# Router logits and ranks issued one level later in a delta-rule recurrence, and a broadcast made by transposes

## The chip, the cores and the metric

The kernel runs on one NeuronCore of a Trainium2 chip. The metric is the device time of one execution in microseconds: the median of 3 runs. The span of a profile is the time from its first to its last instruction. TensorE is called PE here, VectorE DVE, ScalarE ACT, GpSimd POOL and SyncE SP, as in the profile.

## The reference, cut to what matters

x is 4096 tokens of 256 channels, fp32. Four blocks follow one another, each added to x: a delta-rule attention, a mixture of 8 experts with the best 2 of them per token, an RWKV time mix with a channel mix, and a ternary feed-forward net. The change touches the first block and the router of the second:

```
# block 1, per token t (heads fast and slow; the decay per step is a scalar)
pred = (q @ fH + q @ sH) / 2 ; u_neu = sigmoid(sum((v - pred)**2)) > 0.7
fH   = a*fH + (1-a)*(k v^T - k (k @ fH)) ; sH likewise, gated by importance
ns   = ns + u_neu*(nu - ns)*0.1                    # the neuron state
o    = p0*(q @ fH) + p1*(q @ sH) + p2*ns ; x += rmsnorm(o) @ Wo.T
# block 2, the router
logits = layernorm(x) @ w_router ; weights = two largest of softmax(logits)
x += sum over the two chosen experts of weight * mlp_expert(layernorm(x))
```

To send rows to experts the kernel needs, for each token, its logits, its two experts, and its rank among the tokens that chose the same expert (the row it gets in that expert's list).

## The kernel before, in words

**Tiling.** Tokens are cut into 32 chunks of 128 and 8 blocks of 512 (4 chunks). The recurrence is solved chunk by chunk in closed form: within a chunk the inverse of a triangular matrix is applied by 7 levels of repeated squaring. A turn handles two chunks, j = 0 and 1, interleaved; there are 16 turns, u = 0 to 15, from about 100 to 505 us of the span. All code is written out; each engine runs its own list in order, and semaphores alone tie the lists.

**A level on PE** (`level`) is, for j = 0 and then j = 1: four squarings (L1150, L1151), and two multiplications of the matrix into X (L1158, the "X multiplication"). ACT copies the squares out of PSUM (L889), DVE adds the product to X (`apply`, L533). Level 0 of a turn waits, ahead of its first X multiplication, until DVE has done all applies of the turn before:

```
                    elif not first:
                        pe.wait_ge(ap_rdy, t * (2 * LEVELS))
```

**Between the levels** PE does what belongs to the last turn (`y_transposes` L1166, `y_state` L1176, `predict` L1182 to L1186) and to the next (`transposes` L1128, `grams` L1134), and, by a table of stages in `turn`, the work on the block of 512 tokens behind the recurrence. `at(u, parity, lag, stage)` runs a stage in turns of one parity for block (u - lag)/2. In an odd turn: `gate_columns` (L1195) at level 0, `neuron_back` (L1202) and `z1_columns` (L1254) at levels 4 and 5, `logits` (L1212) behind level 6. In an even turn: `o_columns` (L1221) at level 0, `output` (L1230) at level 2, `ranks` (L1240 to L1243) behind level 6. So logits stand at the seam from an odd to an even turn, ranks at the seam from an even to an odd one.

**What they wait for.** `logits` of block b needs both halves of the transposed rows, the second of which ACT copies (`columns`, L943) late in the turn, behind the squares of DVE's new outputs (L911); it also waits until DVE has read bank 5. `ranks` needs DVE to have added the output of the next block (`residual`, L613), which frees bank 7, late in the even turn.

**DVE and ACT.** DVE, in an even turn: apply 0, `fold_words` (L570), `take_logits` (L640), `choose(b, 0)`, apply 1, and so on. In an odd turn: apply 0, `fold_words`, `gates` (L663 to L666), `take_ranks` (L671), `variances` (L625, L627), apply 1. ACT, in an odd turn: squares of level 0, `yt` (L896), `norm_root` (L930, which waits for `variances`), and only then the squares of level 1. At the end of an even turn DVE does `masks` (L520, L523), `residual` (L613), apply 6, `fold_words`, `neuron_gates` (L574, L575) and `stats` (L620); at the end of an odd turn `masks`, `outputs` (L595), apply 6, `fold_words`, `mean_squares` (L601, L602). The multiplications L1134 of `grams` release these masks.

**Behind the turns** stand, in order and on one chain, the last blocks' stages, until POOL has scattered the rows of block 7 (L307) and the experts begin.

Of the kernel before, what the change touches and what calls it, by code (L numbers as in the profile page):

```python
# [16 lines left out]
S, D, DS, HID, NE = 4096, 256, 64, 1024, 8  # L17
CH = 128
# [55 lines left out]
def build(nc, A):  # L74
# [5 lines left out]
    with ctx:  # L80
# [10 lines left out]
        def bank(name):  # L91
            return ctx.enter_context(nc.psum_tensor(name, [128, 512], fp32))
# [14 lines left out]
        def sb(name, shape, dt=fp32, to=None):  # L107
            return (to or ctx).enter_context(nc.sbuf_tensor(name, shape, dt))
# [10 lines left out]
        small = sb("small", [128, 16, NC])  # L119
# [81 lines left out]
        B = [bank(f"bank{i}") for i in range(8)]  # L201
# [80 lines left out]
        NG_, VE, NM, M1, M2, UB, RKU = IMP, RK, RQ, P0, P1, RSTD, RST1  # L282
# [8 lines left out]
        def bank_of(b, item):  # L291

            return (bank_behind if b == LAST else bank_in_turns)[item]


        def block_of(u, parity, lag):

            b = (u - lag) // 2
            return b if u % 2 == parity and u >= lag and b < NB else None
# [754 lines left out]
        def _(pe):  # L1054
            T = nc.tensor
            I_ = ident[:, :]
            pe.wait_ge(mk_rdy, 2)
            for m in range(2):
# [3 lines left out]
                last = T.matmul(B[6][:, 2 + m:3 + m], one_m[0:1, :], pw_s[0:1, m, 128:129], start=True, stop=True)  # L1062
# [11 lines left out]
            def neuron_out(b):  # L1074
                pe.wait_ge(ld_v, 16)
                pe.wait_ge(hd_rdy, b + 1)
                if b >= 1:
                    pe.wait_ge(nu_out, b)
                T.matmul(B[7][0:DS, :], nm2T[:, :], hT[:, :], start=True, stop=True).then_inc(nu_ps, 1)
# [58 lines left out]
            def level(t, p, n, first):  # L1138
                for j in range(2):
                    if n == 0:  # L1140
                        pe.wait_ge(l_rdy, t * 2 + (j + 1))
                        pe.wait_ge(x_rdy, t * 2 + (j + 1))
                    else:
                        pe.wait_ge(sq_cp, t * (2 * LEVELS - 2) + (2 * (n - 1) + j + 1))
                    Ln = L[:, p, j, n % 2, :, :]
                    if n < LEVELS - 1:
                        for m in range(2):
                            a, b_ = Ln[:, 2 * m, :], Ln[:, 2 * m + 1, :]
                            if n < LEVELS - 2:
                                T.matmul(B[j][:, 256 * m:256 * m + 128], b_, a, start=True, stop=True)  # L1150
                            last = T.matmul(B[j][:, 256 * m + 128:256 * m + 256], a, b_, start=True, stop=True)  # L1151
                        last.then_inc(sq_ps, 1)
                    if n > 0:
                        pe.wait_ge(ap_rdy, t * (2 * LEVELS) + (2 * (n - 1) + j + 1))
                    elif not first:
                        pe.wait_ge(ap_rdy, t * (2 * LEVELS))
                    for m in range(2):
                        last = T.matmul(B[2 + j][:, 0:256].rearrange("p (a m d) -> p a m d", a=2, m=2)[:, :, m, :],  # L1158
                                        Ln[:, 2 * m + 1, :], X[:, p, j, :, m, :], start=True, stop=True)
                    last.then_inc(ap_ps, 1)  # L1160

            def y_transposes(t, p):
                pe.wait_ge(ap_rdy, (t + 1) * (2 * LEVELS))
                pe.wait_ge(pp_rdy, t * 2 + 1)
                for j in range(2):
                    last = T.transpose(B[6][:, j * 128:(j + 1) * 128], X[:, p, j, 1, :, :].rearrange("p m d -> p (m d)"), I_)  # L1166
                last.then_inc(yt_ps, 1)
# [3 lines left out]
            def y_state(t, j):  # L1171
                c = t * 2 + j
                pe.wait_ge(yt_rdy, t + 1)
                pe.wait_ge(f_rdy, c + 1)
                pe.wait_ge(pp_rdy, c + 1)
                T.matmul(B[6][:, 256:384], YT[:, j, :], both, start=True, stop=True).then_inc(w_ps, 1)  # L1176

            def predict(t, p, j):
                c = t * 2 + j
                pe.wait_ge(lq_rdy, c + 1)  # L1180
                pe.wait_ge(w_rdy, c + 1)
                T.matmul(B[6][:, 0:128], KQT[:, p, j, 3, :], both, start=True, stop=False)  # L1182
                w = Wb[:, j, :]
                for m in range(2):
                    T.matmul(B[6][:, m * DS:(m + 1) * DS], QM[:, p, j, m, :], w[:, half[m]], start=False, stop=m == 1)
                T.matmul(B[6][:, 384:512], KR[:, p, j, :, :].rearrange("p m d -> p (m d)"), w,  # L1186
                         start=True, stop=True).then_inc(pp_ps, 1)

            def gate_columns(b):
                pe.wait_ge(ng_rdy, b + 1)  # L1190
                if 1 <= b < LAST:
                    pe.wait_ge(x1_rdy, 2 * b - 1)
                for j in range(CPB):
                    c = b * CPB + j
                    last = T.matmul(B[bank_of(b, "gate")][0:DS, j * CH:(j + 1) * CH], small[:, NG_, c:c + 1].broadcast_to([128, DS]), I_,  # L1195
                                    start=True, stop=True)
                last.then_inc(gc_ps, 1)

            def neuron_back(b):
# [6 lines left out]
            def logits(b):  # L1206
                pe.wait_ge(z1T_rdy, 2 * b + 2)
                if b + 1 < LAST:
                    pe.wait_ge(o_rdy, b + 2)
                for j in range(CPB):  # L1210
                    for k in range(KT):
                        last = T.matmul(B[bank_of(b, "logits")][:, j * NE:(j + 1) * NE], zT[:, 0, k, j * CH:(j + 1) * CH], wroT[:, k, :],  # L1212
                                        start=(k == 0), stop=(k == KT - 1))
                last.then_inc(lg_ps, 1)

            def o_columns(b):
                pe.wait_ge(o_rdy, b + 1)
                if 1 <= b < LAST:
                    pe.wait_ge(z1T_rdy, 2 * b)
                for j in range(0, CPB, 2):  # L1220
                    last = T.transpose(B[bank_of(b, "o")][:, j * DS:j * DS + 128], ot[:, j:j + 2, :].rearrange("p c d -> p (c d)"), I_)  # L1221
                last.then_inc(ot_ps, 1)
# [34 lines left out]
            def at(u, parity, lag, stage, *args):  # L1257
                b = block_of(u, parity, lag)
                if b is not None:
                    stage(b, *args)  # L1260

            def turn(u):

                t, p, deltas, head, tail = u, u % 2, u < TURNS, u + 1 < TURNS, 1 <= u <= TURNS
                for n in range(LEVELS):
                    if deltas:
                        level(t, p, n, not tail)
                    if tail:
                        if n == 0:
                            y_transposes(t - 1, 1 - p)  # L1270
                        elif n == 1:
                            y_state(t - 1, 0)
                        elif n == 2:
                            predict(t - 1, 1 - p, 0)
                        elif n == 3:
                            y_state(t - 1, 1)
                        elif n == 4:
                            predict(t - 1, 1 - p, 1)
                    if head:
                        if n in (0, 4):  # L1280
                            transposes(t + 1, 1 - p, n // 4)
                        if n in (2, 5):
                            grams(t + 1, 1 - p, n // 3)
                    if u == 0 and n == 1:
                        neuron_out(LAST)
                        project(NB, 0)
                    if n == 0:
                        at(u, 0, 4, o_columns)
                        at(u, 1, 3, gate_columns)
                    elif n == 2:  # L1290
                        at(u, 0, 4, output)
                    elif n == 4:
                        at(u, 1, 3, neuron_back)
                        at(u, 1, 5, z1_columns, 0)
                    elif n == 5:
                        at(u, 1, 5, z1_columns, 1)
                    elif n == 6:
                        at(u, 1, 5, logits)
                        at(u, 0, 6, ranks)

            z_transposes(0)
            for i in range(NB):
# [20 lines left out]
                turn(u)  # L1323
            t, b5, b6, b7 = TURNS - 1, LAST - 2, LAST - 1, LAST
            y_transposes(t, t % 2)
            o_columns(b6)
            y_state(t, 0)
            predict(t, t % 2, 0)
# [1501 lines left out]
```

## Time and profile before

| | |
|---|---|
| median of 3 runs | 2169.77 us (2169.62 to 2170.21) |
| profiled execution | 2177.72 us, span 2175.9 us |
| PE busy over the span | 90% |
| DVE, ACT, POOL busy | 62%, 45%, 11% |
| mean granted clock of PE | 0.949 |
| the 16 turns | about 100 to 505 us of the span |
| from the turns to the first expert matmul | 505 to 581 us |

The profile is of one execution. Starts and durations of single instructions can be read from its trace; ends of PE instructions are modelled and overlap the next start, so PE's pace is better read from start to start. "Idle before" is the time in which the engine stood still ahead of an instruction, with what released it. The granted clock is 1.00 at 2.4 GHz and 0.50 at 1.2 GHz.

### The profile page before, as it was taken

The page shows a single profiled execution, that of the slowest core. Times are in us where ns is not written, and L with a number is a line of the kernel's source. Part 1 is how long each engine was busy: PE and PEld are TensorE (multiplying, and loading weights), DVE is VectorE, ACT ScalarE, POOL GpSimd, SP SyncE. Part 2 cuts the span into 40 slices and gives each one's busy share as a digit, 9 for nine tenths or more (in the row PEclk, how much of TensorE's full clock was granted, in tenths as well). Part 3 has the DMA queues.
Part 4 walks back from the last instruction along what each step waited for, and adds up shares of the span by engine and source line. Part 5 has one row for each costly group of instructions (what it writes and reads, how often), then busy time and mean ns, then how long its engine had stood idle before and what let it go on. Part 6 is the DMA issues. An engine that isn't in the chain of part 4 may idle for free. (4 is left out here: it accounts for less than half of the span.)

```text
span 2175.9 us, 32550 instructions
## 1 busy us (share of the span) xinstructions
PE 1965.3 (90%) x11554; PEld 1682.8 (77%) x11554; DVE 1354.6 (62%) x2760; ACT 975.4 (45%) x1777; POOL 247.8 (11%) x229
## 2 busy tenths in 40 slices
PE   7999999997399999996776749998999999999999
PEld 5799999996399999996544437776888888888887
DVE  7566677776466666665799877886345345344442
ACT  4655555553234444342788656662232233223221
POOL 0010012222333223232000000000000000000000
PEclk9999999996699999998888869999999999999999
DMA  3299311112444433223232331414000000000000
GB/s 102 85 357 408 113 48 57 57 58 98 154 88 101 87 78 79 49 42 70 69 88 60 94 98 58 174 68 155 1 20 1 19 19 0 20 19 0 20 10 11
DMA packets 86100, 170.36 MB, mean 78 GB/s; under 512 B 7216, under 2 KB 49840, under 8 KB 85808
## 3 DMA queue, kind: packets, MB, share of 16 engines
q1 hardware_dynamic: 65920, 132.47, 17.5%
q0 software_dynamic: 18176, 33.70, 7.7%
q10 hardware_dynamic: 1888, 2.67, 0.4%
q8 instruction: 69, 1.13, 0.2%
q14 instruction: 47, 0.39, 0.1%
HBM read 91.61 MB, written 88.74 MB: 83 GB/s over the span
## 5 line engine op out<-in xcount | busy, mean ns | idle before, releaser
L2642 ACT ACTIVATE x_tok<-bank,scl 128x512 f32<-128x512 f32 x128 | 88.3, 690 | 360.2 <-PE bank L2693 359.4
L2692 PE MATMUL bank<-hAh,ffn_h 128*128 128x512 f32 x512 | 202.7, 396 | 0.7 <-DVE x_tok L2570 0.7
L2692 PE MATMUL bank<-hBh,ffn_h 128*128 128x512 f32 x512 | 201.7, 394 | 0.0
L2693 PE MATMUL bank<-hAl,ffn_h 128*128 128x512 f32 x512 | 199.4, 389 | 0.0
L2693 PE MATMUL bank<-hBl,ffn_h 128*128 128x512 f32 x512 | 199.3, 389 | 0.0
L1475 POOL DMA_INDIRECT tokens_behind_spare_rows<-yg,row_of_token x72 | 133.1, 1848 | 318.5 <-DVE row_of_token L1635 298.3
L889 ACT ACTIVATE L<-bank 128x512 f32<-128x512 f32 x160 | 94.5, 595 | 139.4 <-PE bank L1151 129.6
L533 DVE TENSOR_TENSOR st<-st,bank 128x256 f32<-128x256 f32 x224 | 90.6, 419 | 99.7 <-PE bank L1158 87.6
L1151 PE MATMUL bank<-L 128*128 128x128 f32 x768 | 146.9, 281 | 0.0
L1158 PE MATMUL bank<-st,L 128*128 128x128 f32 x896 | 139.3, 282 | 4.7 <-DVE st L533 4.7
L1572 ACT ACTIVATE h<-bank,b1s 128x256 f32<-128x256 f32 x280 | 125.5, 471 | 36.3 <-PE bank L1403 29.3
L2551 DVE CAST hBh<-x_tok 128x1024 fp32r<-128x1024 f32 x48 | 33.3, 694 | 157.6 <-ACT x_tok L2642 157.0
L1150 PE MATMUL bank<-L 128*128 128x128 f32 x640 | 130.5, 286 | 0.0
L2551 DVE CAST hAh<-x_tok 128x1024 fp32r<-128x1024 f32 x48 | 33.3, 693 | 148.7 <-ACT x_tok L2642 148.2
L1158 PEld LDWEIGHTS bank<-st,L 128*128 128x128 f32 x896 | 120.4, 197 | 6.5 <-DVE st L533 5.2
L1151 PEld LDWEIGHTS bank<-L 128*128 128x128 f32 x768 | 117.3, 197 | 0.1
L1558 ACT ACTIVATE yg<-yt,own_gates 128x256 f32<-128x256 f32 x70 | 31.7, 501 | 183.6 <-DVE yt L1630 176.9
L2692 PEld LDWEIGHTS bank<-hAh,ffn_h 128*128 128x128 f32 x512 | 96.1, 188 | 22.8 <-ACTq L2645 1.4
L2693 PEld LDWEIGHTS bank<-hAl,ffn_h 128*128 128x128 f32 x512 | 96.1, 188 | 21.8 <-issue 1.9
L2692 PEld LDWEIGHTS bank<-hBh,ffn_h 128*128 128x128 f32 x512 | 96.1, 188 | 21.3 <-ACTq L2645 1.4
L2693 PEld LDWEIGHTS bank<-hBl,ffn_h 128*128 128x128 f32 x512 | 96.1, 188 | 21.3 <-issue 1.4
L2692 PE MATMUL bank<-fTh,ffn_w 128*128 128x512 f32 x256 | 100.7, 393 | 6.9 <-ACTq L2615 6.9
(434 smaller groups left out, 5494.7 us busy)
## 6 DMA issues: line engine op xcount, KB each, us to landing
z_by_expert<-zero SPq DMA_DIRECT2D x64, 520.0 KB, 15.8
ckb<-in_ffn_dram POOLq DMA_DIRECT2D x32, 352.0 KB, 3.4
xg<-z_by_expert SPq DMA_DIRECT2D x36, 260.0 KB, 3.1
x_tok<-in_w_dram SPq DMA_DIRECT2D x8, 1024.0 KB
ffn_h<-ffn_copy SPq DMA_DIRECT2D x2, 4096.0 KB, 14.9
x_tok<-after_time_mix SPq DMA_DIRECT2D x15, 512.0 KB, 6.0
st<-in_w_dram SPq DMA_DIRECT2D x6, 1024.0 KB, 6.4
x_tok<-x_T SPq DMA_DIRECT2D x9, 512.0 KB, 4.2
```

What stands on the lines that cost most here:

```text
L533: V.tensor_tensor(x_, x_, B[2 + j][:, 0:256], ALU.subtract if n == 0 else ALU.add).then_inc(ap_rdy, 1)
L889: A_.activation(L[:, p, j, (n + 1) % 2, :, :], src, ACT.Copy).then_inc(sq_cp, 1)
L1150: T.matmul(B[j][:, 256 * m:256 * m + 128], b_, a, start=True, stop=True)
L1151: last = T.matmul(B[j][:, 256 * m + 128:256 * m + 256], a, b_, start=True, stop=True)
L1158: last = T.matmul(B[2 + j][:, 0:256].rearrange("p (a m d) -> p a m d", a=2, m=2)[:, :, m, :], Ln[:, 2 * m + 1, :], X[:, p, j, :, m, :], st ...
L1475: pool.indirect_dma_start(x2_d, bass.IndirectOffsetOnAxis(to_row[:, j:j + 1].bitcast(u32), 0), yg[:, j, :], None, compute_op=ALU.add).then ...
L1558: nc.scalar.activation(yg[:, j, :], yt[:, j, :], ACT.Copy, scale=own_g[:, 0, 0, j:j + 1]).then_inc(y_rdy, 1)
L1572: nc.scalar.activation(h32[:, m, :], B[m % 4][:, 0:TT], ACT.Gelu_apprx_tanh, bias=b1s[:, e * KH + m:e * KH + m + 1]).then_inc(h_act, 1)
L2551: go(V.tensor_copy(dst[0][:, m:m + 2, :], src))
L2642: A_.activation(gq[:, m % 4, :], B[2 + m % 4][:, :], ACT.Gelu, scale=scl[:, off[nm] + m:off[nm] + m + 1]).then_inc(g_act, 1)
L2692: T.matmul(out, w, x[0], start=first, stop=False)
L2693: return T.matmul(out, w, x[1], start=False, stop=last)
```

## The change

`gate_columns` made each of its four 64 x 128 products by a matmul of a broadcast column with the identity; it now makes a 128 x 128 transpose of the column broadcast to 128. ACT still reads the first 64 rows. `logits` moves from behind level 6 of the odd turn to behind level 0 of the next even turn, and `ranks` from behind level 6 of the even turn to behind level 0 of the next odd turn; `logits` of block 5, whose new place would be turn 16, is issued behind the turns. Nothing moves on the other engines.

```
             def gate_columns(b):
...
                     c = b * CPB + j
-                    last = T.matmul(B[bank_of(b, "gate")][0:DS, j * CH:(j + 1) * CH], small[:, NG_, c:c + 1].broadcast_to([128, DS]), I_,
-                                    start=True, stop=True)
+                    last = T.transpose(B[bank_of(b, "gate")][:, j * CH:(j + 1) * CH], small[:, NG_, c:c + 1].broadcast_to([128, 128]), I_)
...
                     if n == 0:
+                        at(u, 0, 6, logits)
+                        at(u, 1, 7, ranks)
                         at(u, 0, 4, o_columns)
                         at(u, 1, 3, gate_columns)
...
-                    elif n == 6:
-                        at(u, 1, 5, logits)
-                        at(u, 0, 6, ranks)
...
             y_transposes(t, t % 2)
+            logits(b5)
             o_columns(b6)
             y_state(t, 0)
```

PE at the seam from an odd to an even turn (turn 5 to turn 6): two pieces of the difference, the end of the odd turn and the place behind level 0 of the even one. The lines of functions further down are numbered one less in the changed kernel, so L1212 is L1211 there.

```order
 L1134 MATMUL bank<-st 128x128 x3
-L1254 MATMUL bank<-ident,Z 128x128 x4
+L1253 MATMUL bank<-ident,Z 128x128 x4
 L1158 MATMUL bank<-st,L 128x2x64 x4
-L1212 MATMUL bank<-small_weights,zT 128x8 x8
 L1150 MATMUL bank<-L 128x128
 L1151 MATMUL bank<-L 128x128
```

```order
 L1166 MATMUL bank<-ident,st 128x128 x2
 L1128 MATMUL bank<-ident,st 128x128 x3
-L1221 MATMUL bank<-ident,big 128x128 x2
+L1211 MATMUL bank<-small_weights,zT 128x8 x8
+L1220 MATMUL bank<-ident,big 128x128 x2
 L1150 MATMUL bank<-L 128x128
```

The last X multiplications of a turn are now followed at once by the squares of the next. The eight logits matmuls stand behind the transposes for the next turn.

PE in the first odd turn that has ranks (turn 7), behind its level 0:

```order
 L1166 MATMUL bank<-ident,st 128x128 x2
 L1128 MATMUL bank<-ident,st 128x128 x3
-L1195 MATMUL bank<-ident,small 64x128 x4
+L1239 MATMUL bank<-mask,tri 128x32
+L1240 MATMUL bank<-seen,one_m 128x32
+L1242 MATMUL bank<-mask,one_m 128x24
+L1242 MATMUL bank<-mask,one_m 128x16
+L1242 MATMUL bank<-mask,one_m 128x8
+L1195 MATMUL bank<-ident,small 128x128 x4
 L1150 MATMUL bank<-L 128x128
```

The five rank matmuls come ahead of the four transposes that replace the four gate matmuls.

PE behind the last turn:

```order
 L1166 MATMUL bank<-ident,st 128x128 x2
-L1221 MATMUL bank<-ident,big 128x128 x2
+L1211 MATMUL bank<-small_weights,zT 128x8 x8
+L1220 MATMUL bank<-ident,big 128x128 x2
 L1176 MATMUL bank<-state,YT 128x128
```

Block 5's logits now stand between the last transposes of Y and the state product that the last two chunks wait for.

## Rows read from the trace of the kernel before

**Rows 1.** Waits of PE, 100 to 505 us: line, releaser, us, times, longest.
```profile
PE bank L1212 <- ACT zT L943: 7.0, 5, 1.4
PE bank L1240 <- DVE x_tok L613: 4.8, 5, 1.0
```

**Rows 2.** Timeline, PE, seam of turns 13 and 14: start, us, line, count.
```profile
446.55 0.93 PE L1134 MATMUL bank<-st 64*128 64x128 f32 x6
...
450.36 1.95 PE L1212 MATMUL bank<-small_weights,zT 128*128 128x8 f32 x16 [1.40 <-ACT zT L943]
452.16 0.47 PE L1150 MATMUL bank<-L 128*128 128x128 f32 x2
...
453.14 0.61 PE L1158 MATMUL bank<-st,L 128*128 128x128 f32 x4
```

**Rows 3.** Timeline, PE, two earlier seams without logits or ranks.
```profile
180.36 0.93 PE L1134 MATMUL bank<-st 64*128 64x128 f32 x6
...
183.89 0.71 PE L1158 MATMUL bank<-st,L 128*128 128x128 f32 x4 [0.62 <-DVE st L533]
...
203.73 0.93 PE L1134 MATMUL bank<-st 64*128 64x128 f32 x6
...
207.29 0.71 PE L1158 MATMUL bank<-st,L 128*128 128x128 f32 x4 [0.64 <-DVE st L533]
```

**Rows 4.** Timeline, PE, first seam with ranks, and two later starts of ranks.
```profile
256.74 0.93 PE L1134 MATMUL bank<-st 64*128 64x128 f32 x6
...
259.73 0.38 PE L1240 MATMUL bank<-mask,tri 128*128 128x32 f32 x2 [0.97 <-DVE x_tok L613]
...
261.81 0.61 PE L1158 MATMUL bank<-st,L 128*128 128x128 f32 x4
...
312.51 0.38 PE L1240 MATMUL bank<-mask,tri 128*128 128x32 f32 x2 [0.97 <-DVE x_tok L613]
...
366.98 0.38 PE L1240 MATMUL bank<-mask,tri 128*128 128x32 f32 x2 [0.97 <-DVE x_tok L613]
```

**Rows 5.** Windows: stretch; length, busy PE, PEld, DVE, ACT, POOL; clock, DMA, GB/s.
```profile
423.40:426.70 3.30, 3.30 (x18) 3.30 (x17) 1.72 (x5) 0.89 (x2) 2.39 (x4) 0.50 0.57 184
```

**Rows 6.** Timelines of PE, DVE and ACT, end of turn 12, start of 13.
```profile
418.43 0.93 PE L1134 MATMUL bank<-st 64*128 64x128 f32 x6
...
421.19 0.74 DVE L533 TENSOR_TENSOR st<-st,bank 128x256 f32<-128x256 f32 x2
...
424.76 0.42 DVE L533 TENSOR_TENSOR st<-st,bank 128x256 f32<-128x256 f32 x1
427.12 0.42 DVE L533 TENSOR_TENSOR st<-st,bank 128x256 f32<-128x256 f32 x1 [1.94 <-issue]
...
430.77 0.21 ACT L930 ACTIVATE small<-small 128x4 f32<-128x4 f32 x1 [1.75 <-DVE small L627]
...
431.58 0.42 PE L1150 MATMUL bank<-L 128*128 128x128 f32 x2
```

**Rows 7.** Timeline, PE, turn 13: the gate's matmuls and four transposes.
```profile
427.56 1.09 PE L1195 MATMUL bank<-ident,small 128*64 128x128 f32 x8
...
444.17 0.66 PE L1254 MATMUL bank<-ident,Z 128*128 128x128 f32 x4
```

**Rows 8.** Timeline, DVE, turn 14: the logits taken, and apply 1.
```profile
456.26 0.18 DVE L640 COPY LG<-bank 128x32 f32<-128x32 f32 x1
...
458.82 0.75 DVE L533 TENSOR_TENSOR st<-st,bank 128x256 f32<-128x256 f32 x2
```

**Rows 9.** Timelines of PE and DVE behind the turns.
```profile
505.65 0.69 PE L1166 MATMUL bank<-ident,st 128*128 128x128 f32 x2 [0.73 <-issue]
...
507.20 0.79 PE L1176 MATMUL bank<-state,YT 128*128 128x128 f32 x2 [0.43 <-ACT YT L896]
...
520.27 0.68 DVE L580 SCALAR_TENSOR_TENSOR big<-bank,NU 64x512 f32<-64x512 f32 x1 [0.16 <-ACT big L907]
...
533.30 3.58 PE L1212 MATMUL bank<-small_weights,zT 128*128 128x8 f32 x16 [0.69 <-ACT zT L943]
```

More of the change, by code:

```diff
@@ L1194, in gate_columns @@
                     c = b * CPB + j
-                    last = T.matmul(B[bank_of(b, "gate")][0:DS, j * CH:(j + 1) * CH], small[:, NG_, c:c + 1].broadcast_to([128, DS]), I_,
-                                    start=True, stop=True)
+                    last = T.transpose(B[bank_of(b, "gate")][:, j * CH:(j + 1) * CH], small[:, NG_, c:c + 1].broadcast_to([128, 128]), I_)
                 last.then_inc(gc_ps, 1)
@@ L1287, in turn @@
                     if n == 0:
+                        at(u, 0, 6, logits)
+                        at(u, 1, 7, ranks)
                         at(u, 0, 4, o_columns)
@@ L1296, in turn @@
                         at(u, 1, 5, z1_columns, 1)
-                    elif n == 6:
-                        at(u, 1, 5, logits)
-                        at(u, 0, 6, ranks)
             z_transposes(0)
@@ L1325, in _ @@
             y_transposes(t, t % 2)
+            logits(b5)
             o_columns(b6)
```

## Prediction, on record before the changed kernel was run

> **What bounds the kernel now.** I read the busy table of the page first: PE leads with 90% of the span. Then the windows over the sixteen turns, then PE's waits there, then timelines around each wait. In the turns PE stands still at few places: 7.0 us ahead of five of the logits groups, for ACT's copy of the transposed rows, and 4.8 us ahead of five groups of ranks, for DVE's residual [rows 1]. Between these, PE is issued without a break, so PE is the bound there and time saved on it is time saved, as long as DVE and ACT follow.
>
> The reader should see a second cost behind the waits. The granted clock of PE falls to 0.50 (1.2 GHz) for 3.4 us and comes back. The windows show five such falls between 230 and 500 us; [rows 5] is one, all 18 PE records of it stretched. One comes 3 us after the first logits wait, the other four about 2 us after the waits of the second to fifth ranks. What one costs is read from the pace: from the first ranks to the second 52.78 us pass without a fall between them, from the second to the third 54.47 us with one [rows 4]; the difference is 1.7 us. I use 1.65, since the other pairs lie at 54.44.
>
> I measure from S, the start of a turn's last Gram group (L1134), because DVE's work at the seam starts from it.
>
> **Seam from odd to even turn (logits), five times.** Before: S is 446.55, the logits start at 450.36 after 1.40 idle and hold PE until 452.16, which is 1.80; the first X multiplication of the next turn starts at 453.14, or S + 6.59 [rows 2]. After: the logits are gone from here, and that multiplication waits for DVE's apply 6. Two earlier seams show this without logits or ranks: S + 3.53 behind `outputs`, with 0.62 idle, and S + 3.56 behind `residual`, with 0.64 idle [rows 3]. So the wait does not vanish; it shrinks and moves into level 0. The logits cost their 1.80 later all the same. Gain: 6.59 - 1.80 - 3.53 = 1.26 each, 5 x 1.26 = 6.3 us. Their data is then long there, as ACT's copy lies ahead of its next squares.
>
> **Seam from even to odd turn (ranks), five times.** Before: from S = 256.74 to the X multiplication at 261.81 is 5.07 [rows 4]. The ranks in it are 10 passes of PE, 1.1 us at the logits' pace (1.80 for 16). After: S + 3.56. Gain at the seam: 5.07 - 1.1 - 3.56 = 0.4. The wait for DVE hardly shrinks, since the same DVE work that delayed the ranks now delays the X multiplication.
>
> **Gate broadcast.** Eight passes last 1.09 us, four transposes in the same stretch 0.66 [rows 7]: a matmul of fp32 is issued as two passes, a transpose as one. With the tail of the last pass, which is paid in either case, taken off, the eight hold PE for about 1.0 and the four for 0.5, so 0.5 is saved per block. In turns 3 and 5, which have no ranks, that is all PE time: 1.0 us. In turn 7 it adds to the 0.4: 0.9 us.
>
> In turns 9 to 15 something else ends last. ACT's copy of the squares of level 1 stands behind L930, which waits for DVE's variances, and those stand behind apply 0, the fold, the gates and the ranks taken. From DVE's second apply of level 0 (427.12) to PE's level 2 (431.58) are 4.46 us, with ACT's L930 at 430.77 in between [rows 6]. After the change DVE sets the pace to there: apply 6 at S + 2.76 (421.19 - 418.43), the first apply of level 0 3.57 later (424.76), the second 0.35 behind it, and then 4.46: S + 11.1. Before it was 431.58 - 418.43 = 13.15 [rows 6], of which 1.65 is the fall of the clock. So 2.0 us are gained where no fall remains, and only 0.35 of these belong to the moved ranks and the gate; DVE takes the rest. Four such turns, the last with a shorter stretch before (12.9): 7.8 us. With turn 7: 8.7 us.
>
> **The clock.** Those 7.8 us contain four falls; the fifth, in turn 6, is 1.65 more. That they go is my choice, and the largest one. What the trace shows is that falls followed long gaps: 1.40 idle, or 0.97 idle with the short rank passes directly behind it, and that the two seams of [rows 3], 0.62 and 0.64 idle, were followed by none. After the change the gaps are 0.4 to 0.9, and full squares and X multiplications (1.8 us) stand between the gap and the short passes.
>
> The Trainium skill speaks against this. "TensorE: Matmul & The Clock Gate", Part 4, says that work in transpose mode does not count as PE being busy for the clock. By that rule the change puts transposes (Y, next turn, gate) right beside the logits and the ranks and makes two stretches per pair of turns that look idle. The z1 transposes of [rows 7] already stand a few us ahead of the logits gap and no fall followed in four of five cases, so the trace leans against it without settling it; what it would do is the last rival below.
>
> **DVE's new wait for the logits.** `take_logits` finds them ready today; afterwards it waits until PE is through level 0, five transposes and the logits, and `choose`, apply 1 and the rest of the turn queue behind it. From the copy to apply 1 are 2.56 us [rows 8], to the end of its first half 3.0. PE needs that half at the X multiplication of level 2: 1.80 of logits, 0.2, a level of 2.7, 0.2 and 0.9 of squares, 5.8 us after the logits begin. DVE gets there 1.95 (duration of the logits in [rows 2]) + 0.1 + 3.0 = 5.05 after. So 0.7 us of cover is left, and I book nothing. `take_ranks` comes behind gates that are later than the ranks: nothing.
>
> **Behind the turns.** Block 5's logits used to run while PE waited for apply 6. Now they lie between Y's transposes (505.65) and the state product (507.20) [rows 9]. At the low clock, which [rows 9] show for the same 16 passes, they take 3.58; less the wait for YT that they cover, 0.43 and part of the 0.6 before it, I take 2.9 us, all on the chain to the experts. Bounds: at full clock 1.8 less 1.1 = 0.7; at the low clock with nothing covered, and a later return of the full clock, 4. The eighth gate is shortened from two passes to one too, but DVE waited only 0.16 for it (L580) [rows 9]: -0.2.
>
> **Sum.** -6.3 - 1.65 - 8.7 - 1.0 + 2.9 - 0.2 = -15.0 us. The profiled execution goes from 2177.7 to 2162.7. It is 7.9 above the median of the runs, which I take as the same for both: 2169.8 - 15.0 = 2154.8, said as 2155. All phases behind are shifted, not changed. About 0.2%, 4.3 us, is what a measurement here can tell from no change.
>
> **Rivals.**
> - *The falls of the clock stay*, one per pair of turns, since gaps remain at every seam. For it: 0.97 idle was enough before, and the even-to-odd gap stays near 0.9. Against: the gap and the short passes are parted. The seams give 6.3 + 5 x 0.4, the gates 1.5 at most where DVE does not hide them, the tail -2.7: 2169.8 - 7 = 2163.
> - *DVE becomes the bound of the even turns.* The 0.7 of cover at `take_logits` is used up where POOL's scatters stretch DVE's small operations, and each of five turns loses about 1 us: 2155 + 5 = 2160.
> - *Slower: two falls per pair.* If stretches with transposes and short passes let the clock fall, both seams of all five pairs have them (the skill's rule as a mechanism of this kernel). Ten falls of 1.65 instead of none: 2154.8 + 16.5 = 2171.3. The point from which it decides is nine falls (15.0 / 1.65). For it: at the odd-to-even seam transposes, logits and o_columns make 2.6 us in a row. Against: 3.2 us of idle and logits in a row caused one fall in five before.
> - *The change does not do what it says*: logits or ranks could be held by another semaphore at the new place. Those they wait for (ACT's copy, DVE's residual and outputs) are all set in the turn before, so I give it no weight of its own.
>
> **Numbers.** Forecast 0.60; falls stay 0.18; DVE-bound even turns 0.12; ten falls 0.05; the rest (a few falls, or other losses behind the turns) 0.05. The forecast's own range is 2151 to 2159, from the bounds of the tail and one fall more. The range for 8 in 10 is 2150 to 2164, which takes in both milder rivals. Faster by over 0.2% is below 2165.4: the first three cases nearly whole, 0.88; within 0.2%: 0.09, most of it the ten falls; slower by more: 0.03.
>
> **What would show it.** In the profile after: no idle ahead of the logits and ranks; 0.4 to 0.9 idle ahead of the first X multiplication of turns 6 to 15, released by DVE L533; the X multiplication at S + 3.5; level 2 of odd turns at S + 11.1; ranks 51.1 us apart; granted clock 1.00 from 130 to 500 us; the gate with 4 records in place of 8; behind the turns the state product 2.9 us later against the turn's end. A clock of 0.50 anywhere in turns 6 to 15, or a PE wait at level 2 of even turns, would make the forecast wrong.

## The result and the profile after

The changed kernel takes 2149.1 us (median of 4 runs, 2148.87 to 2150.3); the kernel before took 2169.99 in the same session (4 runs, 2169.62 to 2170.49). The ratio is 0.9905, with a 95% interval of 0.9888 to 0.9922. So 20.9 us went (by the interval, 17 to 24), where 15.0 were forecast: the direction was right, and the time lies 0.9 us below the lower end of the range. The profiled execution took 2150.3, with a span of 2148.5.

The page of the changed kernel: PE's granted clock in 40 slices of 53.7 us each.

```profile
PEclk9999999995899999997888779999999999999999
```

The turns end in slice 9; the first digit of PEclk below 9, the 5 in slice 10 (483 to 537 us), belongs to the stretch behind them. A window over the turns from 120 us on says it more sharply (columns as in [rows 5]):

```profile
120.00:476.00 356.00, 350.05 (x2994) 337.73 (x2992) 257.14 (x866) 212.01 (x552) 63.82 (x91) 1.00 0.43 157
```

The clock is 1.00 for 356 us; before, five stretches like [rows 5] lay between 230 and 500 us. PE stands still for 6 of the 356 us. The window starts at 120 because one more fall lies ahead of it, in turn 1, with and without the change. PE's waits from 100 to 478 us, which answer to [rows 1]:

```profile
PE bank L1158 <- DVE st L533: 9.0, 13, 3.4
```

The 7.0 us ahead of the logits and the 4.8 ahead of the ranks are gone. What is left is the wait of the first X multiplication for DVE's apply, thirteen times, and 3.4 of the 9.0 is one wait in turn 1; besides it only 0.6 us stand ahead of the last L1253. Timeline of the seam of turns 13 and 14, which answers to [rows 2]; the functions below line 1195 stand one line higher than before, so the logits are L1211 and the ranks L1239:

```profile
426.64 0.93 PE L1134 MATMUL bank<-st 64*128 64x128 f32 x6
...
430.18 0.71 PE L1158 MATMUL bank<-st,L 128*128 128x128 f32 x4 [0.23 <-DVE st L533]
...
432.61 1.85 PE L1211 MATMUL bank<-small_weights,zT 128*128 128x8 f32 x16
...
434.57 0.39 PE L1150 MATMUL bank<-L 128*128 128x128 f32 x2
...
451.76 0.93 PE L1134 MATMUL bank<-st 64*128 64x128 f32 x6
```

The X multiplication starts at S + 3.54 (430.18 - 426.64) and not at S + 6.59; the logits follow without idle. S of turn 12 is 401.32 (below) and S of turn 14 is 451.76, 50.44 later. DVE's take of the logits waits now, and harms nothing:

```profile
434.50 0.19 DVE L640 COPY LG<-bank 128x32 f32<-128x32 f32 x1 [1.01 <-PE bank L1211]
```

The seam of turns 12 and 13, PE, DVE, ACT and POOL, which answers to [rows 4, 6, 7]:

```profile
401.32 0.93 PE L1134 MATMUL bank<-st 64*128 64x128 f32 x6
...
404.87 0.71 PE L1158 MATMUL bank<-st,L 128*128 128x128 f32 x4 [0.64 <-DVE st L533]
...
407.31 0.31 PE L1239 MATMUL bank<-mask,tri 128*128 128x32 f32 x2
...
407.61 0.75 DVE L533 TENSOR_TENSOR st<-st,bank 128x256 f32<-128x256 f32 x2
...
408.34 0.63 PE L1195 MATMUL bank<-ident,small 128*128 128x128 f32 x4
...
408.81 0.39 PE L1150 MATMUL bank<-L 128*128 128x128 f32 x2
...
409.79 0.17 DVE L666 TENSOR_TENSOR Z<-ge,Z 128x4 f32<-128x4 f32 x1
...
410.74 0.20 ACT L930 ACTIVATE small<-small 128x4 f32<-128x4 f32 x1 [1.87 <-DVE small L627]
...
410.85 1.06 ACT L889 ACTIVATE L<-bank 128x512 f32<-128x512 f32 x2
...
411.71 0.39 PE L1150 MATMUL bank<-L 128*128 128x128 f32 x2
```

Here the reader should see that PE's level 2 (411.71) starts without a wait: ACT's first copy behind L930 ends at 411.43 (410.85 + 0.58, the duration of one of the two copies in the group), 0.3 before PE asks for it. It starts at S + 10.39; the prediction said S + 11.1, set by DVE and ACT. That is the step that failed. Behind the turns:

```profile
478.29 0.44 PE L1166 MATMUL bank<-ident,st 128*128 128x128 f32 x2 [0.51 <-DVE st L533]
478.56 1.85 PE L1211 MATMUL bank<-small_weights,zT 128*128 128x8 f32 x16
...
480.52 0.39 PE L1176 MATMUL bank<-state,YT 128*128 128x128 f32 x2
```

The 16 passes of the last block's logits take 1.7 us of PE there, and not the 3.58 of [rows 9]: the clock is still full. The state product is 2.23 behind the Y transposes; in [rows 9] it is 1.55 behind, at the low clock.

### The profile page after: what moved, and what is told of

The parts are those of the page before. It is cut to its first block and busy times, and to the rows that moved or that the text cites. A ratio compares the mean times of both kernels' runs of the same rounds, so it can differ in the third digit from the quotient of the medians.

```text
span 2148.5 us, 32486 instructions
## 1 busy us (share of the span) xinstructions
PE 1951.6 (91%) x11522; PEld 1670.8 (78%) x11522; DVE 1347.8 (63%) x2760; ACT 972.7 (45%) x1777; POOL 247.7 (12%) x229
## 5 line engine op out<-in xcount | busy, mean ns | idle before, releaser
L1151 PE MATMUL bank<-L 128*128 128x128 f32 x768 | 143.7, 276 | 0.0
L1150 PE MATMUL bank<-L 128*128 128x128 f32 x640 | 126.1, 279 | 0.0
```

## Experiments

They ran in three sets, each beside runs of the kernel before on the same chip. That kernel's median was 2173.28 in the first set (21 runs), 2173.37 in the second (7) and 2174.61 in the third (7), some 4 us above the first session, so I compare ratios, or medians within a set. "Pace" is the time from S of one even turn to S of the next. All the traces keep the line numbers to within three.

### First set: the parts alone

**e0, the kernel before again, without an edit.**

> The kernel before, unchanged. Theory: about 8 us of its first profiled execution (2177.7 against runs of 2169.8) are of that execution alone: the first load 2.4 us later than in the changed kernel's profile, and the DVE and ACT waits near 500 and 550 us whose releaser is not named. If so, this profile lies within 2 us of the runs and has none of these waits, while the five falls of PE's clock between 230 and 480 us and the ranks' pace of 54.4 us are there again. Rival: these waits belong to the kernel; then the profile is again about 2177 and shows them, and the change removed them.

Measured: 2172.37 (10 runs, 2169.42 to 2177.9), ratio 1.0 (0.999 to 1.0011). One window with the low clock, and one between this fall and the next:

```profile
232.50:234.50 2.00, 2.00 (x11) 2.00 (x11) 0.42 (x1) 0.60 (x1) 0.00 (x0) 0.50 0.28 113
...
255.00:285.00 30.00, 27.64 (x235) 26.23 (x233) 23.59 (x77) 19.02 (x51) 2.08 (x5) 1.00 0.14 43
```

The same program has five falls again, but all five behind the logits (232, 287, 341, 396 and 450 us), where the first profile had one there and four behind the ranks. So the profile before did not show that the ranks' gap is worse than the logits': in another execution it is the other way. The pace, with one fall in it, is 54.42, as before. The seam of turns 10 and 11 has no fall this time:

```profile
362.64 0.93 PE L1134 MATMUL bank<-st 64*128 64x128 f32 x6
...
369.70 0.42 DVE L533 TENSOR_TENSOR st<-st,bank 128x256 f32<-128x256 f32 x1 [0.33 <-PE bank L1158]
...
371.46 0.17 DVE L666 TENSOR_TENSOR Z<-ge,Z 128x4 f32<-128x4 f32 x1
...
372.41 0.20 ACT L930 ACTIVATE small<-small 128x4 f32<-128x4 f32 x1 [0.81 <-DVE small L627]
...
374.16 0.39 PE L1150 MATMUL bank<-L 128*128 128x128 f32 x2
```

From DVE's second apply of level 0 to L930 are 2.71 us, where [rows 6] had 3.65, and PE comes to level 2 without a wait, at S + 11.52. In [rows 6] it was 13.15, one fall of 1.65 more. Where the fall lies elsewhere, PE's own work ended last there in the kernel before too.

**e1, the gate alone:** only `gate_columns` as in the change.

> Only the gate's broadcast by transposes; logits and ranks stay. Theory: 0.5 us per block in seven turns, all PE time, falls of the clock stay as they are: -3.5 us, 2166.4. Rival (DVE's chain to level 2 ends last in turns 9 to 15, as my prediction had it): only turns 3, 5 and 7 gain, -1.5 us, 2168.4. Rival (transposes do not count as activity for the clock): more falls than five, each +1.65, so 2168 or above with a second fall in odd turns.

Measured: 2172.44 (10 runs, 2168.48 to 2174.82), ratio 0.9995 (0.9985 to 1.0004): nothing. Two of its windows:

```profile
282.60:288.40 5.80, 5.80 (x28) 5.80 (x29) 0.42 (x1) 0.70 (x2) 0.55 (x2) 0.50 0.22 65
445.10:451.10 6.00, 5.83 (x30) 5.83 (x31) 1.32 (x4) 2.24 (x8) 3.72 (x5) 0.57 0.32 107
```

The profile has five stretches of low clock in turns 6 to 15, and these two are about twice as long as the others: seven falls' worth in place of five. From S of turn 5 to S of turn 14 it takes 247.3 us, where e0 takes 245.6. Four shorter gates lie in there, 2.9 us by the 0.73 that e10 shows; two more falls cost 3.3. Another 1.0 is a wait that neither profile of the kernel before has:

```profile
PE bank L1150 <- ACT L L889: 1.0, 2, 0.5
...
372.07 0.49 PE L1150 MATMUL bank<-L 128*128 128x128 f32 x2 [0.53 <-ACT L L889]
```

It stands at level 2 of turns 11 and 13, the two turns from 9 on that have a fall in the seam just before them (364 and 419 us), as [rows 6] have. There PE waits for the chain of the prediction, and the shorter gate brings nearly nothing: level 2 starts at S + 13.06 (S is 359.01) and at S + 12.98, beside 13.15 in [rows 6]. So with a fall in that seam the chain does bind once PE's work is shorter, as the prediction had it. That the other runs of e1 lost their gain in the same way is likely, not shown: only one was profiled.

One more thing differs by chance. All profiles but two have a fall in turn 1, at the wait of 3.4 us; here and in e2 there is none. From S of turn 0 to S of turn 1 pass 25.0 us in these two, 26.6 where the clock is low for 3.4 us (e0, a0, both first profiles), and 27.7 where it is low for 6.8 (e3, e4, e8, e10).

**e2, the ranks alone.**

```diff
                     if n == 0:
+                        at(u, 1, 7, ranks)
...
                     elif n == 6:
                         at(u, 1, 5, logits)
-                        at(u, 0, 6, ranks)
```

> Only the ranks moved behind level 0; logits and gate as before. Theory: the gap of 0.97 and the rank passes directly behind it caused the four falls in turns 9 to 15; parted, they go: 5 x 0.4 + 4 x 1.65 = 8.6, 2161.2, clock 1.00 at the even-to-odd seams. Rival: the falls come from the density of a pair of turns and stay at one per pair: -2.0, 2167.8.

Measured: 2166.16 (6 runs, 2164.41 to 2170.46), ratio 0.9971 (0.9958 to 0.9984). Falls at 230, 285, 340 and 445 us, all behind logits; none at 394, so that 101 us pass at the full clock:

```profile
343.00:444.00 101.00, 96.93 (x824) 92.96 (x824) 75.65 (x258) 61.22 (x159) 20.39 (x28) 1.00 0.17 55
```

S of its even turns:

```profile
361.08 0.93 PE L1134 MATMUL bank<-st 64*128 64x128 f32 x6
...
413.46 0.93 PE L1134 MATMUL bank<-st 64*128 64x128 f32 x6
...
467.47 0.93 PE L1134 MATMUL bank<-st 64*128 64x128 f32 x6
```

52.38 without a fall, 54.01 with one. The kernel before had 52.78 without [rows 4]: the moved ranks are worth 0.40 a pair, and a fall 1.63. So taking the ranks' gap away ended one fall of five. From S of turn 5 to S of turn 14 the profile takes 3.2 us less than e0's, which is four moved ranks and one fall (1.6 + 1.63); the last ranks add 0.4. The missing fall in turn 1 is 1.6 more of this profile. The medians differ by 7.1, and what the runs without a profile did stays open.

**e3, the logits alone.**

```diff
                     if n == 0:
+                        at(u, 0, 6, logits)
...
                     elif n == 6:
-                        at(u, 1, 5, logits)
                         at(u, 0, 6, ranks)
...
             y_transposes(t, t % 2)
+            logits(b5)
```

> Only the logits moved (block 5's behind the turns); ranks and gate as before. Theory: 5 x 1.26 at the seams and the fall in turn 6 gone, 1.65; the four falls at the ranks stay; behind the turns +0.7 if PE's clock is full there, +2.9 if it is low. 2169.8 - 8.0 + 0.7 = 2162.5 at full clock, 2164.7 at the low one. Rival: the falls at the ranks go too, since the logits' wait before them was their cause: 2156.

Measured: 2162.22 (4 runs, 2159.04 to 2164.02), ratio 0.9947 (0.993 to 0.9963). One fall, behind the second ranks, then none for 173 us, though three rank seams with their wait of 0.97 lie in them; the first ranks (256.5 us) had no fall either:

```profile
310.40:313.60 3.20, 3.20 (x17) 3.20 (x17) 1.39 (x4) 1.16 (x2) 2.31 (x3) 0.50 0.49 161
315.00:488.00 173.00, 168.80 (x1439) 161.99 (x1438) 127.11 (x441) 101.99 (x257) 46.61 (x60) 1.00 0.19 61
```

```profile
409.88 0.93 PE L1134 MATMUL bank<-st 64*128 64x128 f32 x6
...
461.44 0.93 PE L1134 MATMUL bank<-st 64*128 64x128 f32 x6
```

The pace is 51.56, so the logits' seam is worth 52.78 - 51.56 = 1.22. Five seams (6.1) and four falls less (6.5) are 12.6, and from S of turn 5 to S of turn 14 the profile takes 12.6 us less than e0's (233.0 and 245.6). The medians differ by 11.1; the fall in turn 1 is the longer one here, 1.1 more. The theory's four falls at the ranks did not stay: one did.

### Second set: the two chains behind the wrong number

**a0, the changed kernel again.**

> The changed kernel, unchanged. It gives the spread of its own executions on this chip. Theory (the times of the kernel before spread over 10 us because its clock falls at other seams in other executions, while the changed kernel has none in the turns): the spread here is below 2 us, against 4 to 10 for the kernel before; median 2149, ratio 0.989 to 0.991. Rival (the spread is of the chip, or of other stages): as wide as before's.

Measured: 2149.38 (4 runs, 2146.09 to 2151.78), ratio 0.9892 (0.9875 to 0.9908). The clock is 1.00 from 120 to 476 us again. Its four runs spread over 5.7 us, those of the kernel before in the same set over 0.9. So the theory failed: falls in turns 6 to 15 are not what makes runs of one kernel differ, as far as the one profiled run tells. By the medians the change is worth 24.0 us in this set (20 to 27 by the interval), beside 20.9 in the first session.

**e4, the last block's logits ahead of the Y transposes:** `logits(b5)` one line higher than in the change.

> The changed kernel with block 5's logits ahead of the last transposes of Y instead of behind them. PE waits there for DVE's last apply (0.5 us) and ACT's copy of the rows is ready 0.4 us before; so the logits cover the wait and then delay Y. By the profile after, the state product starts at 480.65 instead of 480.52: no change, within 0.5 us. My prediction's term (2.9 us lost behind the turns) would have it 2 to 3 us faster; the low-clock variant of it is right if PE's clock falls before the state product in one and not in the other.

Measured: 2150.65 (4 runs, 2149.7 to 2152.29), ratio 0.9897 (0.9881 to 0.9914): no change. From S of turn 14 to the first expert matmul are 95.44 us, beside 95.51 (a0) and 96.25 (first profile after). The kernel before has 98.06 (e0) and 105.07 (its first profile, with 7 us of its own there, one fall among them). The state product starts 28.80 us behind S of turn 14 here, 28.76 in a0, and 29.72 in e0, of which 1.13 are the ranks and the gate of turn 15. So the place of block 5's logits costs 0.2 us at the state product, and which side of the Y transposes they stand on moves nothing.

**e9, longer variances:** blocks 1 to 5 aggregate three times in place of once, 0.82 us more of DVE in the chain to L930, and nothing more for PE.

```diff
-                for c in range(b * CPB, (b + 1) * CPB):
-                    last = V.bn_aggr(mv[:, c, :], st[:, c, :])
-                go(last)
+                for r in range(3 if 1 <= b < LAST - 1 else 1):
+                  for c in range(b * CPB, (b + 1) * CPB):
+                      last = V.bn_aggr(mv[:, c, :], st[:, c, :])
+                  go(last)
```

> The changed kernel, with DVE's bn_aggr of blocks 1 to 5 repeated twice, 0.82 us more of DVE between apply 0 and apply 1 in turns 7 to 15. Theory: ACT's copy of level 1 behind L930 had 0.3 us to spare (copy ends 411.43, level 2 at 411.71), so PE now waits about 0.55 at level 2 in five turns: +2.7 us over the changed kernel, and level 2 starts 10.9 after the last Gram group instead of 10.4. Rival: ACT's order does not bind, DVE's idle time takes it: +0.

Measured: 2155.52 (4 runs, 2154.15 to 2156.9), 6.1 above a0; ratio 0.9918 (0.9902 to 0.9935).

```profile
PE bank L1151 <- ACT L L890: 4.1, 5, 1.6
```

```profile
406.08 0.93 PE L1135 MATMUL bank<-st 64*128 64x128 f32 x6
...
416.12 0.41 DVE L628 TENSOR_SCALAR small<-mv 128x4 f32<-128x4 f32 x1
...
416.57 0.20 ACT L931 ACTIVATE small<-small 128x4 f32<-128x4 f32 x1 [2.95 <-DVE small L628]
...
417.31 0.49 PE L1151 MATMUL bank<-L 128*128 128x128 f32 x2 [0.68 <-ACT L L890]
```

Now the chain is what the prediction took it for: PE waits at level 2, five times, and it starts at S + 11.23. So the chain exists and is only 0.3 us short of binding. L628 takes 0.41 here and 0.17 (as L627) in the changed kernel, which adds to the 0.82. The waits (4.1) do not reach the 6.1 measured, but start to start the trace does: a pair takes 51.39, 0.95 more than 50.44, which makes 3.6 to S of turn 14, and from there to the experts it takes 98.03, 2.5 more than a0, with the longest wait (1.56) in turn 15.

**e8, apply first and the root later:** on top of the change, DVE does apply 6 before the residual and the outputs, and ACT the norm root behind square 1.

```diff
+                if deltas:
+                    apply(t, p, 6)
                 at(u, 0, 4, residual, 1)
                 at(u, 1, 3, outputs)
                 if deltas:
-                    apply(t, p, 6)
...
-                at(u, 1, 5, norm_root)
                 if deltas:
                     square(t, p, 1)
+                at(u, 1, 5, norm_root)
```

> A candidate for a better version: the changed kernel with DVE's apply 6 ahead of residual and outputs, and ACT's norm_root behind the squares of level 1. The waits at the first X multiplication of turns 3 to 15 (5.6 us in the profile after) go, and DVE's later residual is needed only by ranks behind level 0: 2149.1 - 5.6 = 2143.5. Rival: outputs and residual 0.74 us later push ACT's prepare and DVE's apply 0, and PE waits at level 1 or 2 instead: 2149 or slower. Second rival: less idle time but no falls to save, half of the gain: 2146.

Measured: 2146.63 (4 runs, 2145.61 to 2147.7), ratio 0.9877 (0.9861 to 0.9894), the lowest median of all, though its gain over a0 (2.8 us) is within a0's spread, so the runs alone do not show it. The trace does, up to the end of the turns:

```profile
PE bank L1159 <- DVE st L533: 3.4, 1, 3.4
```

The twelve residual waits at the seams are gone and a pair takes 49.47, 0.97 less than in a0. It gives 2.3 us back behind that: 97.84 us from S of turn 14 to the experts, with a new wait ahead of block 5's logits:

```profile
478.15 1.06 PE L1212 MATMUL bank<-small_weights,zT 128*128 128x8 f32 x8 [1.27 <-ACT zT L944]
```

### Third set: what keeps the clock up, and the gate

**e5, transposes added:** on top of the change, 12 more in each of turns 6 to 14 (108 in all), ahead of the logits or the ranks.

```diff
+                for r in range(4 if j == 0 and 6 <= t - 1 < TURNS else 0):
+                    for a in range(3):
+                        T.transpose(B[bk][:, a * 128:(a + 1) * 128], kq_[:, a * DS:a * DS + 128], I_)
```

> The changed kernel with 12 more transposes (the next turn's, repeated into the same bank) directly ahead of the logits or ranks, in turns 7 to 15: 12 passes of PE, 1.34 us each time. With the 5 that stand there, that makes a stretch of 1.9 us of transposes and then 1.1 or 1.8 us of short passes. Theory (transposes keep the clock up as matmuls do): no fall, 9 x 1.34 = +12.1 over the changed kernel. Rival (the Trainium skill, TensorE: Matmul & The Clock Gate, Part 4: transpose mode does not count as busy): a fall of 3.4 us in most of these turns, up to 9 x 1.65 = 15 more, +20 to +27, and the granted clock 0.50 there.

Measured: 2161.72 (4 runs, 2157.59 to 2163.6), ratio 0.9936 (0.9918 to 0.9955).

```profile
120.00:490.00 370.00, 363.80 (x3120) 351.50 (x3119) 260.24 (x870) 214.32 (x555) 64.03 (x92) 1.00 0.42 154
```

```profile
412.40 0.93 PE L1137 MATMUL bank<-st 64*128 64x128 f32 x6
...
465.46 0.93 PE L1137 MATMUL bank<-st 64*128 64x128 f32 x6
```

The clock stays at 1.00. A pair takes 53.06, 2.62 more than 50.44, which is 0.11 for each of its 24 transposes: their own time and nothing else.

**e6, the same place and PE time as matmuls:** `range(2 ...)` and `T.matmul(..., start=True, stop=True)`, six of two passes each.

> The control: the same place and the same 12 passes, but as 6 fp32 matmuls with the identity. Both theories: no falls, +12.1 over the changed kernel; only if the short passes of logits and ranks matter and not the transposes would it show the same falls as the kernel with transposes.

Measured: 2163.2 (4 runs, 2159.95 to 2166.59), ratio 0.9952 (0.9935 to 0.997). No fall in the turns either, and a pair takes 53.12, beside 53.06. Transposes and matmuls behave alike here.

**e10, both moves with the old gate.**

```diff
-                    last = T.transpose(B[bank_of(b, "gate")][:, j * CH:(j + 1) * CH], small[:, NG_, c:c + 1].broadcast_to([128, 128]), I_)
+                    last = T.matmul(B[bank_of(b, "gate")][0:DS, j * CH:(j + 1) * CH], small[:, NG_, c:c + 1].broadcast_to([128, DS]), I_,
+                                    start=True, stop=True)
```

> Both moves, with the gate's broadcast by matmuls as before. Theory: with no falls left for the phase to play with, the gate is worth its PE time, 0.5 us in seven turns and little behind them: 2149.4 + 3.5 = 2152.9, pairs of turns 50.9 us apart instead of 50.4. Rival: it is worth nothing, as when it was changed alone (2172.4 against 2173.3): 2149.4 to 2150.2.

Measured: 2156.85 (4 runs, 2154.68 to 2160.96), ratio 0.9915 (0.9898 to 0.9931).

```profile
409.24 0.93 PE L1134 MATMUL bank<-st 64*128 64x128 f32 x6
...
460.41 0.93 PE L1134 MATMUL bank<-st 64*128 64x128 f32 x6
```

The pace is 51.17. Against 50.44 the gate is worth 0.73 a turn, in seven turns 5.1 us, beside 5.0 by the ratios (0.9915 and a0's 0.9892, whose intervals overlap). With both moves and the old gate no fall is left in the turns, so the shorter gate is now pure PE time; alone (e1) it moved nothing.

**e11, e8 with e4's edit.**

> The version with DVE's apply 6 first and norm_root later, and with block 5's logits ahead of the last Y transposes. Theory: the loop as in the version without that last edit, pairs 49.5 us apart, and the stretch from the last Gram group of turn 14 to the first expert work shorter by up to 0.8: 2146. Rival: the low clock behind the turns, which comes at another moment, decides that stretch: 2146 to 2149.

Measured: 2148.82 (4 runs, 2147.78 to 2150.55), ratio 0.9879 (0.9863 to 0.9896). It does not beat e8: PE waits longer for ACT's transposed rows ahead of block 5's logits, 2.2 us in place of 1.27.

## Why the prediction was right in direction and short in size

In the turns the parts add up without a remainder. A pair of turns without a fall takes 52.78 before; less 1.22 (e3), 0.40 (e2) and 0.73 (e10) is 50.43, and the changed kernel takes 50.44. From S of turn 5 to S of turn 14 a0 takes 18.8 us less than e0, which is five logits' seams, four of the ranks, four gates and five falls.

- **Logits' seams, -6.3.** Right: 1.22 each where 1.26 were booked, and the wait shrinks and moves to the X multiplication at S + 3.5, as said. Only the idle time left there is 0.23, below the 0.4 to 0.9 named as a sign, as the z1 transposes (L1253), which the turns of [rows 3] do not have, fill part of it.
- **Ranks' seams, 0.4 each.** Right: 0.40, with a wait of 0.64 left.
- **The falls go, five times 1.65.** Right in sum and size: none between 120 and 476 us, twice; the pace with one differs by 1.63 from the pace without in e2. Wrong in the reason, so that the term came true is in part luck: the falls were tied to the ranks' gap of 0.97 with short passes behind it. e0 has all five behind the logits and e3 keeps four such gaps of ranks without a fall. What is shown is narrower, for turns 6 to 15: with both waits in a pair (first profile, e0, e1) five falls, five, and seven falls' worth; with the logits' wait alone four (e2, one profile); with the ranks' alone one (e3, one profile); with neither none, in all nine profiles that have both moves. The length of a single wait does not decide: in e9 PE waits 1.56 in turn 15 (469.25) and the clock stays at 1.00 for 18 us more, and the wait of 3.4 in turn 1 had no fall behind it in e1 and e2. What picks the seam in one execution stays open.
- **Odd turns 9 to 15, 2.0 each: the failed step.** The prediction let DVE's and ACT's chain end last, "S + 11.1", and gave it the gate and the ranks: "only 0.35 of these belong to the moved ranks and the gate; DVE takes the rest". All of it counted: 0.40 + 0.73 + 1.65 = 2.8 in place of 2.0, 3.2 us in four turns, and level 2 starts at S + 10.39 without a wait. The 4.46 from DVE's second apply to level 2 [rows 6] was read as the chain's length and carried over into turns without a fall. In e0 the same 4.46 (369.70 to 374.16) are PE's own, with L930 0.9 us sooner behind the apply. [Rows 6] name no wait of PE at 431.58, a sign that PE's own work ended last there too, if only by 0.1 us: ACT's first copy starts at 430.88 and takes 0.58. In e0 the same copy is done 1.06 before PE asks (372.52 + 0.58, and 374.16). The chain had been nearly as long as PE's work only because of the fall: the fall had set DVE back against POOL, and two of DVE's small operations met POOL's multiplication:

```profile
429.09 0.62 DVE L666 TENSOR_TENSOR Z<-ge,Z 128x4 f32<-128x4 f32 x1
429.21 0.47 POOL L347 TENSOR_TENSOR st<-st,lamr 128x128 f32<-128x128 f32 x1
...
430.29 0.44 DVE L627 TENSOR_SCALAR small<-mv 128x4 f32<-128x4 f32 x1
```

  In e0 and in the changed kernel L666 and L627 take 0.17 each. From the apply to L930 are 3.65 here, 2.71 and 2.78 there. e1 keeps the fall in that place, and the chain binds there (S + 13.06 in turn 11, with a wait of 0.53 and L666 0.63 long); e9 shows that without a fall it binds only once it is 0.8 longer. So the prediction took the fall's 1.65 off PE's work and kept the chain that the fall had stretched.
- **The gate, 0.5 each.** Too low: 0.73. From its start to the next instruction's it shrinks from 1.02 (427.56 to 428.58) to 0.47 (408.34 to 408.81), which is 0.55. The rest stands at its two edges. In turn 3, before and after:

```profile
161.37 0.49 PE L1128 MATMUL bank<-ident,st 128*128 128x128 f32 x3
...
163.13 0.39 PE L1151 MATMUL bank<-L 128*128 128x128 f32 x2
```

```profile
159.03 0.49 PE L1128 MATMUL bank<-ident,st 128*128 128x128 f32 x3
...
160.02 0.39 PE L1151 MATMUL bank<-L 128*128 128x128 f32 x2
```

  That is 1.76 and 0.99. Of the 0.77, 0.09 lie in the three transposes ahead (start to start 0.42 and 0.33), 0.58 in the group (1.02 and 0.44) and 0.10 in the two passes behind (0.32 and 0.22). Only the old group has the form 128\*64 in its row [rows 7], and the passes around it 128\*128; that this change of form is what costs at the edges is likely, not shown. Between e10 and a0, in turn 13, the three pieces are 0.07, 0.55 and 0.10, which is the 0.73. Over turns 3, 5 and 7 this is 0.7 us.
- **Behind the turns, +2.9.** Too dear: 0.2 at the state product (e4), which is 2.7 us. The price came from [rows 9], 28 us behind the Y transposes of that profile and at the low clock; at its place behind the turns the clock was still full. From S of turn 14 to the experts a0 takes 2.55 us less than e0 and the first profile after 1.8 less, where 1.13 belong to turn 15, so that another 0.9 to 1.6 us were gained behind the state product; this is not followed further.
- **Cover at `take_logits`.** Right: DVE waits 1.01 for the logits, and level 2 of the even turns never waits.

Sum of the misses: 3.2 + 0.7 + 2.7 = 6.6, and 15.0 + 6.6 = 21.6, beside 20.9 measured in the first session, 24.0 in the second, and 21.8 between the spans of e0's and a0's profiles. The first session's interval alone reaches from 17 to 24, so these sums cannot be told apart. For the term behind the turns the dear one of two values had been taken.

The last rival fell. The Trainium skill's "TensorE: Matmul & The Clock Gate", Part 4, says that transpose mode does not count as PE-busy the same way for the clock. In e5, with 17 transposes (1.9 us) ahead of each group, the granted clock is 1.00 over 370 us, and the added transposes cost their own 0.11 us each, as e6's matmuls do. For fp32 transposes in this kernel the measurement speaks against that sentence; a longer stretch of transposes was not run.

## What to carry to other kernels

Before a chain of other engines is made the bound of a step, look whether the bottleneck engine's row carries a wait there: without one, the interval measured is that engine's own, and what is taken from it counts as far as the other chain ends earlier. Read that slack from the end of the last copy ahead: here 0.1 us in the turn with a fall, where the shorter gate brought 0.1, and 1.06 without, where it brought all. Do not carry a chain's length from a turn with a fall of the clock into one without. Where short waits cost falls, count them per pair of stages and remove both: without the ranks' wait four of five falls stayed, without the logits' one, without both none, and the saving of the gate alone was eaten by falls and by the chain. Take a second profile of the kernel before, if there can be one: here it would have shown that the seam of the fall and the stretched DVE operations were chance.

## What the runs showed of the hardware

- A fall of TensorE's granted clock from 2.4 to 1.2 GHz for 3.4 us, behind a wait of 1 to 1.4 us, costs 1.63 to 1.7 us (e2, [rows 4]). Where it falls differs between executions of the same program (first profile, e0), and at the same wait of 3.4 us in turn 1 the clock is low for 0, 3.4 or 6.8 us, which costs 0, 1.6 or 2.7 (e1 and e2; e0; e3).
- The profile of e1, with shorter PE work alone, has seven falls' worth of low clock in turns 6 to 15 in place of five, and its ratio is 0.9995. That the shorter work brought them is not shown.
- DVE operations on 128x4 elements (L627, L666) take 0.17 us with no multiplication of POOL beside them, and 0.43 to 0.63 beside its multiplication of 128x128 (first profile, e1). In e9 one takes 0.41 with that multiplication starting as it ends (416.58), so what stretches it there stays open.
- An fp32 transpose of 128x128 holds PE for 0.11 us and leaves one record; four of them in place of four fp32 matmuls of 64 rows with eight records save 0.73 us a turn: 0.55 in the group, and 0.07 and 0.10 at its edges (e10, a0).
